# A graph layer, a linear-attention mix and a routed FFN on one core: the edge loop's transposed one-hot moves from TensorE and ACT to DVE, register loads are batched, and routing starts before the last update

## What is computed

```python
xn = layernorm(x)                                  # x: (3125, 256)
# graph layer, 50000 edges (ei = src, ej = dst), one weight each
msg = silu(concat(xn[ei], xn[ej], weight) @ mW1 + mb1)
msg = silu(layer_norm(msg, ln_g, ln_b) @ mW2 + mb2)
agg = segment_sum(msg, ei)
gnn = xn + silu(concat(xn, agg) @ uW1 + ub1) @ uW2 + ub2
# mix: 8 heads of 64, k and v normalised, q @ (k^T v) / n, output projection
x = x + gnn + mix(xn)
# FFN: layernorm, router to 8 experts, top 2, softmax over the two
x = x + sum over the two chosen experts of w * (gelu(z @ W1[e] + b1[e]) @ W2[e] + b2[e])
```

## Time and profile before

| | us |
|---|---|
| median of 3 runs | 1616.63 (1613.83 to 1616.96) |
| profiled execution | 1614.69 |
| its span (first to last instruction) | 1612.9 |
| TensorE, DVE, ACT, POOL busy, share of the span | 89%, 74%, 61%, 52% |
| edge loop | 407 to 1206 |
| updates | 1229 to 1303 |
| routing | 1303 to 1324 |
| slot lists and w_rest | 1324 to 1356 |
| expert slots | 1356 to 1585 |
| final sum | 1585 to 1613 |

### The profile page before, as it was taken

The page is one execution under the profiler, slowest core; times in us unless marked ns, Lnnn a source line. Parts: engine busy times, 40 slices in busy tenths (PEclk is TensorE's granted clock), DMA queues, the critical chain, the costliest instruction groups (busy, mean ns, idle before and its releaser), DMA issues.

```text
span 1612.9 us, 34882 instructions
## 1 busy us (share of the span) xinstructions
PE 1431.6 (89%) x8790; PEld 1183.5 (73%) x8791; DVE 1186.1 (74%) x4460; ACT 981.2 (61%) x2146; POOL 839.8 (52%) x1203
## 2 busy tenths in 40 slices
PE   4565999979899999999999999999998945999991
PEld 2454665556799999999999999998996633777771
DVE  7999436652899999989999999989993466444442
ACT  1342224431688888888888888888884252666560
POOL 1487750014366666666666666666640002666651
PEclk7655999989799999999999999999999977999996
DMA  7400120001122222222222222222733062444437
GB/s 193 90 4 5 46 59 1 1 23 56 40 75 73 74 73 72 73 73 74 72 72 72 74 73 73 74 72 72 73 66 138 1 230 83 66 68 65 71 56 255
DMA packets 63010, 118.03 MB, mean 73 GB/s; under 512 B 21729, under 2 KB 41473, under 8 KB 62450
## 3 DMA queue, kind: packets, MB, share of 16 engines
q0 software_dynamic: 36560, 77.33, 20.7%
q1 hardware_dynamic: 25616, 36.80, 7.2%
q10 hardware_dynamic: 780, 3.24, 0.5%
HBM read 92.57 MB, written 24.72 MB: 73 GB/s over the span
## 4 chain that ended last, share of the span: by engine, by line
PE 78%; DVE 13%; ACT 4%; issue 3%; DMA 2%; DVEq 0%; ACTq 0%; POOLq 0%
PE ps L937 13%; PE ps L692 9%; PE ps L1029 6%; PE ps L917 6%; PE ps L907 5%; PE ps L824 5%; PE ps L904 4%; PE ps L899 4%; PE ps L900 4%; PE ps L788 3%; DVE place_val_t L1392 3%; PE ps L927 2%; DVE lane_hot_e_t L1387 2%; PE ps L1056 2%; PE ps L1055 2%
## 5 line engine op out<-in xcount | busy, mean ns | idle before, releaser
L640 POOL DMA_INDIRECT msg_t<-dst_table,stage_idx x448 | 446.9, 998 | 107.6 <-issue 46.3
L937 PE MATMUL ps<-msg_t,hot_t 128*125 128x256 f32 x896 | 241.5, 392 | 13.7 <-issue 7.4
L1160 ACT ACTIVATE msg1n_t<-msg_t,nw_b,nw_y 128x256 f32<-128x256 f32 x448 | 243.7, 598 | 0.0
L1177 ACT ACTIVATE msg_t<-msg_t 128x512 f32<-128x512 f32 x224 | 141.5, 632 | 100.9 <-DVE msg_t L1572 100.8
L899 PE MATMUL ps<-w_hi_t,msg1T_hi_t 128*128 128x256 f32 x672 | 198.5, 310 | 0.0
L606 POOL DMA_INDIRECT sorted_edges<-sort_sb_t,chunk_to x112 | 136.0, 1214 | 86.2 <-DVE chunk_to L1379 52.7
L900 PE MATMUL ps<-w_lo_t,msg1T_hi_t 128*128 128x256 f32 x672 | 179.8, 282 | 0.0
L937 PEld LDWEIGHTS ps<-msg_t,hot_t 128*125 128x125 f32 x896 | 151.2, 188 | 31.8 <-issue 9.6
L917 PE MATMUL ps<-src_hi_t,hotT_t 127*128 x448 | 160.8, 379 | 3.7 <-ACT hotT_t L1173 3.7
L1572 DVE TENSOR_TENSOR msg_t<-ps,msg_t 128x512 f32<-128x512 f32 x224 | 152.5, 681 | 3.4 <-PE ps L917 3.4
L904 PE MATMUL ps<-w_hi_t,msg1T_lo_t 128*128 128x256 f32 x672 | 153.6, 283 | 0.0
(11 more groups left out here) (346 smaller groups left out, 3569.5 us busy)
## 6 DMA issues: line engine op xcount, KB each, us to landing
w_sb_t<-in_L_ffn_W_dram SPq DMA_DIRECT2D x16, 512.0 KB, 7.9
msg_t<-dst_table,stage_idx POOLq DMA_INDIRECT x448, 2.8
res_t<-in_x_dram SPq DMA_DIRECT2D x1, 3125.0 KB
total<-zero_chunks_t SPq DMA_DIRECT2D x1, 3125.0 KB, 39.4
dst_table<-dst_stage SPq DMA_DIRECT2D x25, 125.0 KB
xm_table<-xm_t POOLq DMA_DIRECT2D x5, 625.0 KB, 7.4
total<-res_t SPq DMA_DIRECT2D x1, 3125.0 KB
sum_b_t<-total ACTq DMA_DIRECT2D x5, 625.0 KB, 11.2
```

Source lines behind the costliest of these rows:

```text
L640: pool.indirect_dma_start(out=msg1[:, k, j, :], out_offset=None, in_=dst_table, in_offset=bass.IndirectOffsetOnAxis(stage_idx[:, half, q:q ...
L937: m = pe.matmul(bank(7, D, rows=NP), hot[:, (k - 8) % TURN, j, 0:NP].bitcast(F32), msg2[:, k % 2, j, :], start=(j == 0), stop=(j == G - 1))
L1160: m = A(msg1n[:, (k + 1) % 2, j, :], msg1[:, kk, j, :], ACT.Identity, bias=nw_b[:, kk, j:j + 1], scale=nw_y[:, kk, j:j + 1])
L1177: A(v, v, ACT.Silu).then_inc(msg1_sb, 1)
```

## The change

- `hotT` is made on DVE, directly: a TENSOR_SCALAR compares `near_rows` (the row number of each edge, broadcast to all partitions, fp16) with the partition's own number `row_col`. TensorE's L927 and ACT's L1173 go. `near_rows` comes by SP, five units per DMA, out of a list in DRAM that is written before the loop; the edge weights come by SP into rows 125 and 126 of `hotT` (90 DMAs in all); POOL's `edge_weights` goes.
- `hot` (L1592 after) is built for unit n − 7 in two buffers, later in the step.
- All four quarters of the second layer are split: no `msg1T_f`, and hi and lo have 512 columns.
- The sums alternate between PSUM banks 0 and 7.
- DVE reads ten block numbers in one TENSOR_LOAD at k = 0; TensorE 4, 3 and 3. Two turns instead of one are unrolled ahead of the loop (`FROM`); a shift `LAG` exists and is 0.
- Routing: logits are copied per block, spreads, logits, max and max_index are taken per chunk between the updates; the root is POOL's `pow`; the normalised rows are made (ACT) and stored earlier; the counts are summed over 8 columns (`row_n`) and not 400; the scan stands ahead of TensorE's sums.
- TensorE waits for `w_rest` in the first slot's second layer and not before the first slot; the store of `totals[0]` is two DMAs.

```diff
@@ TensorE, edge step @@
-                        split = [c for c in range(KD) if c * UE + j * 128 < SPLIT]
+                        for c in range(KD):
...
-                        if len(split) < KD:
-                            m = pe.matmul(o[j], msg1T_f[:, (k + 1) % 2, :], w2c[:, KD - 1, :], start=False, stop=True)
-                if k == 0:
-                    load_blocks(mybir.EngineType.PE, blk, n, 0, 3)
+                if k in (0, 4, 7):
+                    load_blocks(mybir.EngineType.PE, blk, n, k, 4 if k == 0 else 3)
...
-                    for j in range(G):
-                        m = pe.matmul(bank(0, 128, rows=HR, first=j * 128), hot[:, (k + 1) % TURN, j, 0:HR], ident_r[:],
-                                      start=True, stop=True)
-                    m.then_inc(hotT_ps, 1)
...
-                        m = pe.matmul(bank(7, D, rows=NP), hot[:, (k - 8) % TURN, j, 0:NP].bitcast(F32), msg2[:, k % 2, j, :],
+                        m = pe.matmul(bank(7 * (kl % 2), D, rows=NP), hot[:, kl % 2, j, 0:NP], msg2[:, kl % 2, j, :],
@@ ACT, edge step @@
-                    A(msg1T_hi[:, k % 2], bank(3 + k % 2, SPLIT), ACT.Copy)
-                    A(msg1T_f[:, k % 2], bank(3 + k % 2, 128, first=SPLIT), ACT.Copy).then_inc(msg1T_sb, 1)
+                    A(msg1T_hi[:, kl % 2], bank(3 + kl % 2), ACT.Copy).then_inc(msg1T_sb, 1)
...
-                    A(hotT[0:HR, (k + 1) % 2, :], bank(0, UE, rows=HR), ACT.Copy).then_inc(hotT_sb, 1)
@@ DVE, edge step @@
-                    dve.tensor_tensor(hot[:, kk, :, 0:NP], iota[:, 1:NP + 1].unsqueeze(1).broadcast_to([128, G, NP]),
-                                      rows.broadcast_to([128, G, NP]), ALU.is_equal).then_inc(hot_ready, 1)
+                    dve.tensor_scalar(hotT[0:NP, kk, :], near_rows[kk // NEAR][0:NP, kk % NEAR, :], row_col[0:NP, :], None,
+                                      ALU.is_equal).then_inc(hotT_sb, 1)
                 if k == 0:
-                    load_blocks(mybir.EngineType.DVE, blk, n - 9, 0, 4)
+                    load_blocks(mybir.EngineType.DVE, blk, late - 9, 0, TURN)
...
-                    dve.tensor_tensor(msg1T_lo[:, k % 2], bank(3 + k % 2, SPLIT),
-                                      msg1T_hi[:, k % 2].bitcast(F32), ALU.subtract)\
+                    dve.tensor_tensor(msg1T_lo[:, kl % 2], bank(3 + kl % 2), msg1T_hi[:, kl % 2].bitcast(F32), ALU.subtract)\
                        .then_inc(msg1T_lo_sb, 1)
                 rstd_step(first_q + 2, slot, pair_on)
+                m_ = late - 7
+                if here(m_, UNITS):
+                    after(dve, sum_ps, m_ - 1)
+                    rows = recs[:, bass.ds(G * m_, G), 1:2]
+                    dve.tensor_tensor(hot[:, (kl + 1) % 2, :, 0:NP], iota[:, 1:NP + 1].unsqueeze(1).broadcast_to([128, G, NP]),
...
-                if k in (1, 5):
-                    load_blocks(mybir.EngineType.DVE, blk, n - 6, k + 3, 4 if k == 1 else 2)
@@ SP @@
+            for h, m in enumerate(range(0, UNITS, NEAR)):
+                some = min(NEAR, UNITS - m)
+                if h >= 2:
+                    sp.wait_ge(hotT_sb, m - NEAR)
+                sp.dma_start(near_rows[h % 2][:, 0:some, :].rearrange("p k e -> p (k e)"),
+                             row_list[m * UE:(m + some) * UE].partition_broadcast(128)).then_inc(near_in[h % 2], 16)
@@ DVE, between the updates and after them @@
+                if c >= 2:
+                    pick(c - 2)
+                if 1 <= c < len(CH) - 1:
+                    spread_of(c - 1)
...
-            dve.wait_ge(sd2_ok, 1)
-            step(dve.reciprocal(rstd[R], rstd[R]))
-            dve.scalar_tensor_tensor(nbias[R], meanvar[R, :, 0], -1.0, rstd[R], ALU.mult, ALU.mult).then_inc(rstd2_ok, 1)
...
+            spread_of(len(CH) - 2)
+            spread_of(len(CH) - 1)
+            for t in range(NB - 3, NB):
+                raw_logits(t)
+            pick(len(CH) - 2)
+            pick(len(CH) - 1)
@@ TensorE, routing @@
-            pe.matmul(bank(3, NE * KT, rows=NP), earlier[0:NP, 0:NP], flat, start=True, stop=True)
-            pe.matmul(bank(4, NE * KT, rows=NP), ones[0:NP, 0:NP], flat, start=True, stop=True).then_inc(route_ps, 1)
+            pe.matmul(bank(3, NE, rows=NP), earlier[0:NP, 0:NP], row_n[0:NP, :], start=True, stop=True)
+            pe.matmul(bank(3, NE, rows=NP, first=NE), ones[0:NP, 0:NP], row_n[0:NP, :], start=True, stop=True)\
+              .then_inc(route_ps, 1)
```

More of the change, by code:

```diff
@@ L58, in gps_layer @@
     FIELDS = 3
+    LAG = 0
+    NEAR = 5
     PIECES = 6
@@ L661, in _, with store_rows @@
                       allow_small_or_imprecise_dtypes=True).then_inc(token_ok, 1)
-            for g in range(5):
+            def store_rows(g):
                 pool.wait_ge(xm_ok, 5 * (g + 1))
@@ L665, in _ @@
                                xm[0:NP, 5 * g:5 * g + 5, :]).then_inc(xm_out, 16)
+            for c in range(len(CH)):
+                T = slice(CH[c][0], CH[c][-1] + 1)
+                pool.wait_ge(var2_ok, c + 1)
+                pool.tensor_tensor(rstd[0:NP, T], rstd[0:NP, T], minus_half[0:NP, 0:len(CH[c])], ALU.pow).then_inc(sd2_ok, 1)
+                if c >= len(CH) - 3:
+                    store_rows(c - len(CH) + 3)
+            for g in range(3, 5):
+                store_rows(g)
             def fetch(n):
@@ L831, in turn_records @@
             def turn_records(g):
-                for v in range(FIELDS):
+                for v in range(2):
                     m = turn(bank(RECS[g], LT, first=v * LT),
@@ L893, in edge_step @@
                     after(pe, msg2_sb, m_ - 1)
-                    o = [bank(5 + (k + 1) % 2, D, first=j * D) for j in range(G)]
-                    part = lambda t, j, c: t[:, (k + 1) % 2, c * UE + j * 128:c * UE + j * 128 + 128]
+                    o = [bank(5 + (kl + 1) % 2, D, first=j * D) for j in range(G)]
+                    part = lambda t, j, c: t[:, (kl + 1) % 2, c * UE + j * 128:c * UE + j * 128 + 128]
                     for j in range(G):
-                        split = [c for c in range(KD) if c * UE + j * 128 < SPLIT]
-                        for c in split:
+                        for c in range(KD):
                             pe.matmul(o[j], part(msg1T_hi, j, c), w2_hi[:, c, :], start=(c == 0), stop=False)
@@ L975, in route @@
                 pe.wait_ge(x2T_sb, t + 1)
+                after(pe, logit_ok, t)
                 for k in range(KD):
@@ L1614, in add_hidden, with raw_logits, spread_of, pick @@
                 m.then_inc(hid_pre, 1)
+            def raw_logits(t):
+                if t >= 0:
+                    dve.wait_ge(logit_ps, t + 1)
+                    dve.tensor_copy(logits[R, t, :], bank(7, NE, rows=NP, first=t * NE)).then_inc(logit_ok, 1)
+            def spread_of(c):
+                T = slice(CH[c][0], CH[c][-1] + 1)
+                st.join()
+                dve.tensor_scalar(rstd[R, T], meanvar[R, T, 1], 1.0 + EPS, EPS * EPS, ALU.mult, ALU.add).then_inc(var2_ok, 1)
+            def pick(c):
+                blocks, n = CH[c], len(CH[c])
+                T = slice(blocks[0], blocks[-1] + 1)
+                dve.wait_ge(sd2_ok, c + 1)
+                dve.wait_ge(logit_ok, blocks[-1] + 1)
+                dve.scalar_tensor_tensor(nbias[R, T], meanvar[R, T, 0], -1.0, rstd[R, T], ALU.mult, ALU.mult)\
+                   .then_inc(rstd2_ok, 1)
+                step(dve.tensor_tensor(logits[R, T], logits[R, T], rstd[R, T].unsqueeze(2).broadcast_to([NP, n, NE]), ALU.mult))
+                step(dve.tensor_tensor(logits[R, T], logits[R, T], logit0[R].unsqueeze(1).broadcast_to([NP, n, NE]), ALU.add))
+                for t in blocks:
+                    st.did(dve.max(top_v[R, t, :], logits[R, t, :]))
+                st.join()
+                for t in blocks:
+                    st.did(dve.max_index(top_e[R, t, :], top_v[R, t, :], logits[R, t, :]))
             dve.wait_ge(mixed_ok, NB)
```

295 lines of the change are left out of this document (153 added, 142 removed).

## The result

The changed kernel takes 1668.97 us (1665.97 to 1670.99, 4 runs) against 1616.45 of the kernel before on the same chip: ratio 1.0327, 95% interval 1.0306 to 1.0348. The forecast was 1669. The profiled execution took 1670.32, with a span of 1668.6 against 1612.9.

The account below looks back on a forecast made before the run. It took TensorE (3.51 us a step) as the bound before, a DVE–ACT ring of 3.68 after. Loop +65, start +2, drain −0.6, routing and first slot −13.7 sum to +52.7 on 1616.63: 1669 us, range 1635 to 1702.

Parts of the forecast that it names:

- The ring: Edge loop, DVE to ACT to DVE: lo to add 1.81, add to lo 1.87, 3.68 us a step, above TensorE's 3.27.
- Ten values: DVE's register load at k = 0: ten block numbers last 2.28 us, 1.32 more than four.
- rival A: DVE's load: ten values cost like four, each turn 1.32 us shorter, 1640 us in all; chance 0.12.
- The step with the load: Edge loop at k = 0: 1.81 + 4.12 = 5.93 us, once a turn of 39.05.
- the 2.88 from add to lo of the kernel before: Step with DVE's load of four: 2.88 + 1.32 − 0.08 (hotT for hot) = 4.12 us after the change.
- rival C: Edge loop: TensorE's clock falls behind each stall, 1.7 us a turn, up to 1706 us; chance 0.10.
- rival B: Edge loop: hotT and POOL's gathers hold each other up, 1695 us in the middle, 1709 at most; chance 0.07.
- Routing and first slot: Behind the edge loop: shorter routing and an earlier first slot_h, together −13.7 us (−11 to −16).
- the rest go where DVE waits for TensorE: Routing: max and max_index, except five blocks behind the last update, move into DVE's waits; −3.3 us.
- Start and drain: Around the edge loop: first add 2 us later (+1 to +4), drain 0.6 us shorter.
- not under 0.86: Edge loop, a sign of the forecast: TensorE busy for under 0.86 of the loop.

Follow-up runs that it names:

- experiment 2: Changed kernel with the lines of hot moved from between lo and the add to right behind hotT: 1627.85 us, ratio 1.0104.
- Experiment 8: Kernel before with only the fourth quarter of the second layer split like the others, lo and hi 512 wide: 1622.34 us, ratio 1.0041.
- experiment 5: Changed kernel with the third group of record-table transposes back on TensorE, their result read by nobody: 1669.38 us, ratio 1.0333.
- experiment 6: Changed kernel with the raw logit copy of each chunk's first block ahead of the next chunk's hidden adds on DVE: 1665.21 us, ratio 1.0299.

## Why the prediction was right

*The ring.* Forecast 1.81 + 1.87 = 3.68 a step; measured 1.81 + 1.86 = 3.67. That it is a ring, and not DVE's sum, experiment 2 shows: moving hot, nothing else, took 1.9 us off a turn. Experiment 8 fits the other half of it, that in the kernel before the ring lay close under TensorE's step: with 0.13 more on DVE and 0.07 less on TensorE a turn grew by 0.36. The way from the one to the other is argued there.

*hotT* lasts 0.32 to 0.35, with the overlap of 0.08 the 0.26 forecast, and hides: in every other unit lo still waits for hi by 0.23 behind it. *Ten values* last 2.29 us for 2.28 forecast; rival A is out. The step with the load was forecast at 5.93 and is 5.68. The term that was mis-sized is the 2.88 from add to lo of the kernel before, onto which the 1.32 was put: it holds an idle time of 0.14 ahead of hot (904.49 to 904.63), and hotT has none; the other 0.1 is not traced. The steps next to the one with the load take 3.74 and 3.75 instead of 3.68, so that the turn is 38.89 for 39.05. That makes 0.16 × 21.8 = 3.5 of the 6.6 us by which the loop came out shorter than forecast. Most of the rest lies in the first twenty steps, which grew by 1.7 us over those of the kernel before and not by some 4.

*TensorE's clock* in the loop is 0.99: rival C didn't come. TensorE's idle time behind the load was not one piece of 2.7 but 0.62 before the lo products and 1.37 before the next transposes. Ahead of the loop it was another matter: from 346 us the clock stayed at 0.50, and two groups of 8 and 16 matmuls (L877, L883) took 3.65 and 5.77 us where L844 and L850 had taken 1.91 and 3.72. That waits for data are followed by slow matmuls is what the Trainium skill describes ("TensorE: Matmul & The Clock Gate", section "HAM oscillation — how this bites in real kernels"); the traces agree at 343 to 346 us, behind a wait of 2.98, in nine of the ten profiles of this chip; they don't in that of experiment 5, with the same wait, and not behind the loads in the loop. *Gathers* were no longer than before (963 ns each for 998): no rival B.

*What failed*, in the step "Routing and first slot": "the rest go where DVE waits for TensorE". Their work does hide, but the raw copies became a wait of TensorE's route, and one of them per chunk stands behind the hidden adds; +5.1 on the updates (1229.90 to 1302.25 before, 1292.47 to 1369.94 after), of which experiment 6 gives back 2.7 in the traces (3.8 in the medians). The other 2.4 stand behind the last chunk's copy of sums, where nothing was tried: between the last block's add (1366.97) and its last statistics (1369.94) DVE does the max and max_index of four blocks, and from the one to the other it takes 2.97 us, for 1.19 before. And in "Start and drain" nothing was foreseen ahead of the loop, where +3.3 came. The parts that came out worse (+3.3, +0.6 at the first add, +5.1, and routing's −7.1 instead of −8.7) and those that came out better (the loop by 6.6, the drain by 1.1) nearly cancel. That the time met the forecast to the microsecond is luck; the parts are off by up to 6.6.

TensorE's busy share in the loop is 752.52 of 853, 0.88, not under 0.86.

## What to carry to other kernels

When two engines hand one buffer back and forth within a step, add up the ring as well as each engine's work: a step inside the ring lengthens it by its whole length (0.34 for hot, lo to add 1.81 against 1.47), and the same step beside the wait costs only what exceeds the wait. Look at what the ring lacks under the bounding engine's step before you bring the two together: experiment 8, which did, lost more in one step a turn than it gained in the others. Put register loads where the engine waits anyway, in pieces as short as that wait, and look at those of the bounding engine first: in the kernel before, the two steps with TensorE's own loads are 0.9 us a turn longer than the plain ones.
